# One draining step fewer between slot attention and cross attention in a fused decoder layer

## The reference

```
x = x + gated_slot_attention(layernorm(x))          # 4 heads, 64 slots
x = x + cross_attention(layernorm(x), ctx, bias)    # 16 heads of width 8
x = x + experts(layernorm(x))                       # 8 experts by LoRA, 2 chosen
# cross attention, for one batch:
scores = q k^T / sqrt(8) + attn_mask + 2 * fside    # fside: 16 x 128 x 128 per batch
scores = where(key_mask, -inf, scores)
out    = softmax(scores) v, times Wo, plus bo
```

## Time and profile before

| | us |
|---|---|
| median of 3 runs | 661.64 |
| lowest, highest | 657.6, 661.92 |
| the profiled execution: its time | 662.49 |
| its span, first to last instruction | 660.7 |
| busy: PE, DVE, ACT, POOL | 540.4, 520.1, 439.0, 366.2 |

### The profile page before, as it was taken

How to read it: one execution, slowest core, us unless ns; L and a number is a source line. 1 busy time by engine, 2 the same in 40 slices (tenths; PEclk the granted TensorE clock), 3 DMA queues, 4 the chain that set the end, 5 groups by cost and what they waited for, 6 DMA issues and landing times. The chain is left out here.

```text
span 660.7 us, 16042 instructions
## 1 busy us (share of the span) xinstructions
PE 540.4 (82%) x4272; PEld 403.4 (61%) x4272; DVE 520.1 (79%) x2036; ACT 439.0 (66%) x1569; POOL 366.2 (55%) x365
## 2 busy tenths in 40 slices
PE   3589999999999765887877887877866799999986
PEld 1357777777777643555555555555545677777764
DVE  1446878888788635999999999999986699999872
ACT  3655787787776214999999999999994232223321
POOL 5123454453543457888888888888842134333430
PEclk9778999999999755999999999999997699999999
DMA  5930000000000034788887788888700000000000
GB/s 127 213 51 1 2 0 2 0 0 0 0 1 1 3 71 83 136 152 150 148 144 136 140 153 148 151 145 141 132 2 1 0 17 16 17 16 16 17 17 16
DMA packets 87510, 42.37 MB, mean 64 GB/s; under 512 B 7466, under 2 KB 87220, under 8 KB 87476
## 3 DMA queue, kind: packets, MB, share of 16 engines
q1 hardware_dynamic: 87476, 41.97, 34.8%
HBM read 39.86 MB, written 2.10 MB: 64 GB/s over the span
## 5 line engine op out<-in xcount | busy, mean ns | idle before, releaser
L957 ACT ACTIVATE c_P<-c_P,c_min 128x128 f32<-128x128 f32 x512 | 222.0, 648 | 0.0
L957 ACT ACTIVATION_READ_ACCUMULATOR c_P<-c_P,c_min 128x1 f32 x512 | 186.8, 447 | 0.0
L1126 POOL TENSOR_TENSOR c_bias<-c_fside,c_cm 128x2048 f32<-128x2048 f32 x32 | 145.5, 4546 | 3.0 <-DVE c_cm L1043 3.0
L1018 DVE CUSTOM_DVE_ANT_0 c_P<-banks,c_bias 128x128 f32<-128x128 f32 x512 | 117.1, 286 | 7.3 <-issue 4.3
L913 PE MATMUL banks<-ident,c_P 128*128 128x128 f32 x512 | 84.1, 289 | 28.7 <-ACT c_P L957 26.1
L913 PEld LDWEIGHTS banks<-ident,c_P 128*128 128x128 f32 x512 | 57.5, 145 | 47.9 <-ACT c_P L957 31.9
L1053 DVE COPY shared<-banks 128x512 f32<-128x512 f32 x96 | 66.0, 687 | 2.8 <-PE banks L913 2.8
L1468 POOL TENSOR_TENSOR xs<-shared,xs 128x512 fp32r<-128x512 f32 x8 | 10.8, 1349 | 94.9 <-ACT xs L1300 94.9
L1233 PE MATMUL banks<-um,lb_s 128*128 128x512 f32 x192 | 56.4, 409 | 2.7 <-ACT shared L1290 1.9
L1290 ACT ACTIVATE shared<-banks,bi_col 128x512 f32<-128x512 f32 x32 | 22.0, 688 | 46.0 <-PE banks L1233 46.0
L766 POOL TENSOR_TENSOR lower<-meanvar,minus_one 128x2 f32<-128x2 f32 x16 | 3.1, 197 | 80.8 <-DVE meanvar L647 80.5
(11 more groups left out here) (195 smaller groups left out, 1451.5 us busy)
## 6 DMA issues: line engine op xcount, KB each, us to landing
c_fside<-in_fside_Bx16xSxS_dram SPq DMA_DIRECT2D x64, 512.0 KB, 7.2
X<-in_x_dram SPq DMA_DIRECT2D x4, 512.0 KB, 4.9
c_ctx<-in_ctx_dram SPq DMA_DIRECT2D x32, 64.0 KB, 5.2
out_dram<-shared SPq DMA_DIRECT2D x8, 256.0 KB, 2.3
kmask_sb<-in_mask_BxS_bf_dram SPq DMA_DIRECT2D x1, 512.0 KB, 6.9
c_P<-in_L_ffn_wi_dram SPq DMA_DIRECT2D x1, 256.0 KB
c_P<-in_L_ffn_wo_dram SPq DMA_DIRECT2D x1, 256.0 KB
c_P<-in_L_ffn_lora_B_dram SPq DMA_DIRECT2D x4, 64.0 KB
```

The lines of the kernel that those rows point to most:

```text
L957: last = nc.scalar.activation(P[:, par, h, :], P[:, par, h, :], ACT.Exp, bias=mn[:, par, h:h + 1], scale=-1.0, accum_out=rsx[:, par, h:h + 1])
L1018: last = nc.vector.tensor_tensor_reduce(out=P[:, o, h, :], in0=bank(SCORE_BANKS[i])[:, 128 * j:128 * j + 128], in1=fm[:, o, h, :], scale=- ...
L1126: nc.gpsimd.tensor_tensor(fm[:, q, :, :], fs[:, q, :, :], bc(cm[:], XH), ALU.add).then_inc(C["fm"], 1)
```

## The change

- The bias tile of batch 0 is made between slot steps 5 and 6, that of batch 1 between slot steps 14 and 15, by new functions `x_masks` (DVE) and `x_biases` (POOL) in place of the inner `masks` and `biases`. On DVE the masks stand before the loop (after step 5) and after it (before step 14).
- Cross step -3 moves ahead of slot step 16, cross -2 ahead of 17, cross -1 ahead of 18.
- In cross steps below 0, POOL does `roots` first, then `keys_apart` and the output bias, and no bias tile.
- Slot step 18 is cut: its DVE part without `mean_squares`, and POOL's squares, before cross step 0; `mean_squares` and `root` of the last pair after cross step 0; slot step 19 after cross step 1 (POOL has nothing in it).
- The fourth group of scores of batch 0 goes to bank 0 in place of bank 6; the transposes of cross step -1 then wait until all its scores are read (`C["tt"]` >= 4).

```diff
+        FIRST_BANKS = (1, 4, 5, 0)
+        def score_bank(n, i):
+            return bank((FIRST_BANKS if isinstance(n, int) and n == 0 else SCORE_BANKS)[i])
+        def x_masks(dve, k):
+            need(dve, C["fm"], k)
+            km = kmask_sb[:, bass.ds(k * T, T)]
+            nc.vector.scalar_tensor_tensor(cm[:], km, -3.0e38, half_mask[:], ALU.mult, ALU.add).then_inc(C["cm"], 1)
+        def x_biases(pool, k, m, q):
+            need(pool, C["cm"], k + 1)
+            need(pool, s_fs[q], 32 * (m + 1))
+            need(pool, C["tt"], 4 * k - 4)
+            nc.gpsimd.tensor_tensor(fm[:, q, :, :], fs[:, q, :, :], bc(cm[:], XH), ALU.add).then_inc(C["fm"], 1)
@@ x_tensor, inputs_turned
+                if isinstance(n, int) and n == -1:
+                    need(pe, C["tt"], NI)
@@ x_vector
-            if project:
-                masks()
+            if project and not (isinstance(n, int) and n < 0):
+                x_masks(dve, n + 2)
@@ x_pool
+            if isinstance(n, int) and n < 0:
+                if norm:
+                    roots()
+                if project:
+                    keys_apart()
+                    output_bias()
+                return
@@ gpsimd
             for t in range(1, 6):
                 gsa_peeled(gsa, t)
+            x_biases(pool, 0, 0, 0)
             gsa_loop(pool, gsa)
-            for t in range(PAIRS - 2, PAIRS + 1):
-                gsa_peeled(gsa, t)
+            gsa_peeled(gsa, PAIRS - 2)
+            x_biases(pool, 1, 0, 1)
+            gsa_peeled(gsa, PAIRS - 1)
             pool.wait_ge(G["xn"], PAIRS)
             x_peeled(cross, -3)
-            gsa_peeled(gsa, PAIRS + 1)
+            gsa_peeled(gsa, PAIRS)
...
             x_peeled(cross, -2)
-            gsa_peeled(gsa, PAIRS + 2)
+            gsa_peeled(gsa, PAIRS + 1)
             x_peeled(cross, -1)
-            gsa_peeled(gsa, PAIRS + 3)
-            for n in range(0, 2):
-                x_peeled(cross, n)
+            gsa(PAIRS + 2, 0, False, False, False, True, False, False, False)
+            x_peeled(cross, 0)
+            gsa(PAIRS + 2, 0, False, False, False, False, False, False, True)
+            x_peeled(cross, 1)
@@ vector
             for t in range(4, 6):
                 gsa_peeled(gsa, t)
+            dve.wait_ge(s_km, 16)
+            x_masks(dve, 0)
             gsa_loop(dve, gsa)
-            for t in range(PAIRS - 2, PAIRS + 1):
+            x_masks(dve, 1)
+            for t in range(PAIRS - 2, PAIRS):
                 gsa_peeled(gsa, t)
...
             x_peeled(cross, -3)
+            gsa_peeled(gsa, PAIRS)
+            x_peeled(cross, -2)
             gsa_peeled(gsa, PAIRS + 1)
-            dve.wait_ge(s_km, 16)
-            x_peeled(cross, -2)
-            gsa_peeled(gsa, PAIRS + 2)
             x_peeled(cross, -1)
+            gsa(PAIRS + 2, 0, False, False, False, True, True, False, False)
+            x_peeled(cross, 0)
+            gsa(PAIRS + 2, 0, False, False, False, False, False, False, True)
+            x_peeled(cross, 1)
             gsa_peeled(gsa, PAIRS + 3)
             dve.wait_ge(G["x1"], PAIRS)
-            for n in range(0, 2):
-                x_peeled(cross, n)
             x_loop(dve, cross)
@@ tensor
-            x_peeled(cross, -3)
-            gsa_peeled(gsa, PAIRS + 1)
             pe.wait_ge(G["silu"], PAIRS)
             x_peeled(cross, -2)
+            gsa_peeled(gsa, PAIRS + 1)
+            pe.wait_ge(G["shift"], PAIRS)
+            x_peeled(cross, -1)
             gsa_peeled(gsa, PAIRS + 2)
-            pe.wait_ge(G["lgts"], PAIRS)
             pe.wait_ge(G["un"], PAIRS)
-            x_peeled(cross, -1)
+            pe.wait_ge(G["onT"], PAIRS - 1)
+            pe.wait_ge(G["x1"], PAIRS - 1)
+            x_peeled(cross, 0)
+            x_peeled(cross, 1)
...
             gsa_peeled(gsa, PAIRS + 3)
             pe.wait_ge(G["x1"], PAIRS)
```

More of the change, by code:

```diff
@@ L647, in gsa_stats, with gsa_vector @@
                 nc.vector.bn_aggr(meanvar[:, b, :], stats[:, b, :]).then_inc(G["aggr"], 1)
-        def gsa_vector(dve, t, par, gate, turn, intra, mix, finish, ahead):
+        def gsa_vector(dve, t, par, gate, turn, intra, mix, finish, ahead, squares=None):
             def log_sigmoid():
@@ L754, in gsa_vector @@
                 slot_sums()
-            if mix:
+            if mix if squares is None else squares:
                 mean_squares()
@@ L773, in gsa_rstd, with gsa_pool @@
             nc.gpsimd.tensor_tensor(neg_mean[:, 0:2], lower[:, 0:2], rstd[:, 0:2], ALU.mult).then_inc(G["neg"], 1)
-        def gsa_pool(pool, t, par, gate, turn, intra, mix, finish, ahead):
+        def gsa_pool(pool, t, par, gate, turn, intra, mix, finish, ahead, norms=None):
             def heads_apart():
@@ L813, in gsa_pool @@
                 squares()
+            if mix if norms is None else norms:
                 root()
@@ L870, in all_scores @@
                     rows = slice(32 * i, 32 * i + 32)
-                    nc.tensor.matmul(bank(SCORE_BANKS[i]), qx[rows, o, :], kbd[rows, o, :, :].rearrange("p j s -> p (j s)"),
+                    nc.tensor.matmul(score_bank(n + 1, i), qx[rows, o, :], kbd[rows, o, :, :].rearrange("p j s -> p (j s)"),
                                      start=True, stop=True).then_inc(C["sc"], 1)
@@ L1017, in score @@
                     h = XG * i + j
-                    last = nc.vector.tensor_tensor_reduce(out=P[:, o, h, :], in0=bank(SCORE_BANKS[i])[:, 128 * j:128 * j + 128],
+                    last = nc.vector.tensor_tensor_reduce(out=P[:, o, h, :], in0=score_bank(n + 1, i)[:, 128 * j:128 * j + 128],
                                                           in1=fm[:, o, h, :], scale=-2.0, scalar=3.0e38, op0=ALU.add,
@@ L1037, in normalise @@
                                         ALU.subtract, ALU.mult).then_inc(C["xn"], 1)
[L1039 to L1043, removed]
             def outputs():
@@ L1119, in roots @@
                 nc.gpsimd.tensor_tensor(rstd[:, 0:1], vareps[:, 0:1], minus_half[:, 0:1], ALU.pow).then_inc(C["rstd"], 1)
[L1121 to L1126, removed]
             def keys_apart():
@@ L1677, in _ @@
                 gsa_peeled(gsa, t)
-            x_peeled(cross, -3)
-            gsa_peeled(gsa, PAIRS + 1)
             pe.wait_ge(G["silu"], PAIRS)
             x_peeled(cross, -2)
+            gsa_peeled(gsa, PAIRS + 1)
+            pe.wait_ge(G["shift"], PAIRS)
+            x_peeled(cross, -1)
             gsa_peeled(gsa, PAIRS + 2)
-            pe.wait_ge(G["lgts"], PAIRS)
             pe.wait_ge(G["un"], PAIRS)
-            x_peeled(cross, -1)
+            pe.wait_ge(G["onT"], PAIRS - 1)
+            pe.wait_ge(G["x1"], PAIRS - 1)
+            x_peeled(cross, 0)
+            x_peeled(cross, 1)
+            pe.wait_ge(C["ptD"], 6)
+            pe.wait_ge(C["ptA"], 2)
             gsa_peeled(gsa, PAIRS + 3)
             pe.wait_ge(G["x1"], PAIRS)
-            for n in range(0, 2):
-                x_peeled(cross, n)
             x_loop(pe, cross)
```

6 lines of the change are left out of this document (5 added, 1 removed).

## The result

| | median us | lowest to highest, runs | profiled run | span | first L726 to end of span |
|---|---|---|---|---|---|
| before, same session | 659.62 | 656.42 to 661.92, 4 | 662.49 | 660.7 | 595.5 |
| after | 672.72 | 671.99 to 673.12, 4 | 671.99 | 670.2 | 610.7 |

The ratio is 1.0196, interval 1.0144 to 1.0248: slower by 1.4 to 2.5%, 13.1 us by the medians where I had forecast 5.6 (667.2 us).

What follows compares the result with a forecast made beforehand. The loops leave little room (PE busy in slots, ACT in the cross loop); open time lies in the drain. -2.0 drain + 0.1 batch 3 + 0.2 masks + 4.3 hold + 3.0 clock = +5.6, so 667.2 us; range 657.5 to 674.5.

Steps and rivals of the forecast that it cites:

- the forecast case: Whole kernel: drain gives 2.0 us, slot 15's L726 is held and PE's clock falls; 661 to 671 us, chance 0.63.
- Tile 0 holds L726 too: Rival, slot 6: batch 0's tile starts before L726, so 4.3 + 3.0 us come a second time; 674.5 us, chance 0.14.
- the 0.1 for batch 3: After the drain: 0.1 us left for batch 3's scores, which start only after slot 19.
- The hold: Slot 15: batch 1's tile starts first on POOL and DVE's L726 is held until it ends; 4.3 us, bounds 0 and 4.5.
- Tile 1 hides: Rival, slot 15: batch 1's tile does not hold DVE's L726; 660.1 us, chance 0.18.
- The clock behind it: Slot 15, after held L726: PE idles, its granted clock falls to 0.50; 3.0 us, bounds 0 and 6.
- Tile 0: Slot 6: DVE's L726 starts before batch 0's bias tile and keeps 0.42 us; masks cost DVE nothing visible.
- The drain: Steps between slot and cross loops: sum 63.0 us against 65.0 before, a gain of 2.0, bounds 0 and 6.
- Cross -3: 1.9 is its full price: Drain: cross -3 keeps 1.9 us, but DVE, PE and ACT now all wait for it.
- Slot 16: 10.2, same work: Drain: slot 16, now behind cross -3, keeps its 10.2 us because its work is unchanged.
- Cross -1: 8.75: Drain: 8.75 us instead of 8.4; L871, the scores, then transposes, projections and values follow one after the other.
- Slot 19: 2.55: Drain: 2.55 us instead of 3.35, as its PE legs run at the high clock that returns in cross 0.

Runs made afterwards that it cites:

- e2: Changed kernel with PE's `mix` matmuls of slot step 15 issued five times over, same output: 667.2 us; 606.8 from first L726 to end.
- e3: Changed kernel with batch 1's bias tile made in two halves, heads 0 to 7 before L726, 8 to 15 behind: 669.0 us; 602.2 from first L726.
- e11: Same program as e1, run again for its startups: 661.1 us (2 runs) and 668.9 (4); 600.0 from first L726 to end.
- e6: e1 with slot 18 whole and slot 19 ahead of cross 0, as in the kernel before: 658.0 and 665.9 us by group, ratio 1.0010.
- e9: Changed kernel with the edits of e1, e5 and e6 together: 656.3 and 661.3 us by group, ratio 0.9963; 596.4 from first L726.
- e7: Kernel before with roots first in cross -2 and -1, batch 0's tile after slot 18's L726, batch 1's right after the roots: median 656.1 us, ratio 0.9954.
- e8: e7 with layer-norm statistics and roots of cross -2 and -1 laid inside slots 16 and 17: median 654.17 us, ratio 0.9939.
- e1: Changed kernel with one added wait: POOL makes batch 1's bias tile only after L726 of slot 15. Median 669.91 us, ratio 1.0154.
- e4: Kernel before with roots first in cross -2 and -1, batch 0's tile behind them, batch 1's after slot 19's L726: 661.78 us, ratio 1.0014.
- e5: e1 with layer-norm statistics and roots of cross -3 and -2 laid inside slots 15 and 16: 658.2 and 662.1 us by group, ratio 1.0008.

## Why the prediction was right, and where not

**The number: in the range, in part by luck.** 672.7 lies within 657.5 to 674.5, but outside the 661 to 671 that I gave the forecast case itself; the range reached so far only for the sake of the rival *Tile 0 holds L726 too*, which did not happen. Laid beside the 15.2 us of the traces, my +5.6 is 9.6 short: 0.9 in the clock behind the hold, 6.4 in the drain, 1.9 in the first loop step (2.0 against the 0.1 for batch 3), 0.4 behind it.

**The hold: right, in place and size.** Forecast: tile 1 starts first at L794's end and L726 ends with it, 4.3 us. Measured: tile 190.28, L726 190.35 to 195.06, and 4.3 by e2. What was inferred from holds of 0.6 and 1.1 us goes on to 4.5, and e3 shows it in between. The Trainium skill ("SBUF — State Buffer", Who interferes with whom), by which the first to start has the shared read port for its whole instruction, agrees. *Tile 1 hides* is out.

**The clock behind it: right, sized 3.0, measured 3.9** (e2). Granted 0.50 from 194 to 202 as forecast, and 0.69 up to 204, so it reached L701 too (its wait on ACT, behind slow PE, rose from 1.0 to 2.02).

**Tile 0: right.** At slot 6, L869 at 83.04 lets both go, L726 starts at 83.24 and takes 0.42, the tile at 83.40. The measured time lies near that rival's 674.5, but not by its mechanism. A slip that changed nothing: the rows I took for this place, at 63 to 70 us, belong to slot step 4. A second one: I said that `masks` is held by L794 to its end. It is not: in the kernel before L1043 starts at 244.62, inside L794, and takes its usual 0.28. On POOL:

```profile
244.45 1.64 POOL L794 TENSOR_TENSOR shared<-shared,minus_half 128x8 f32<-128x8 f32 x1 [0.73 <-DVE shared L720]
```

So the rule that I drew from L715 and L1404, that a DVE instruction with two inputs in SBUF is held until the POOL instruction beside it ends, is true of the add and multiply tiles here and not of this power of 8 numbers.

**The drain: the step that failed.** I summed 63.0 and measured 69.4, and forecast -2.0 where it is +4.4, with 2.0 more in the first loop step. Term by term:
- *"Cross -3: 1.9 is its full price"* and *"Slot 16: 10.2, same work"*. Cross -3 is 1.87, but it pauses PE, and slot 16 is 13.43, by 3.2 the largest miss. I charged the clock for the pause of 4.3 us and not for that of 1.9. e11 shows what the clock is worth: the same program with the clock left up takes 9.35 there. That the pause brings the fall is the likely reading (five of seven profiles with it, none of two without), but not a fixed rule.
- *Cross -1: 8.75*. It is 10.04. Start and scores together take about what I gave them (5.4 against 5.3, up to PE's first transpose at 245.06), and so do the legs from the transposes to the end of the projections, which I had read at the low clock (2.4 against 2.3, up to 247.46). What was mis-sized is the rest, "plus the values and copies": 1.1 in my sum, 2.2 measured. The values wait for ACT's copies of queries and keys, DVE's copy waits for the values, and only then come L1055 and the next L726, at 249.66:

```profile
246.83 0.63 PE L909 MATMUL banks<-c_cT,x_wT 128*128 128x128 f32 x2
248.18 0.80 PE L921 MATMUL banks<-x_wT,c_cT 128*128 128x128 f32 x2 [0.72 <-ACT c_k L992]
249.01 0.29 DVE L1086 COPY c_vpad<-banks 128x128 f32<-128x128 f32 x1 [4.11 <-PE banks L921]
```

- *Slot 17: 11.4* was 12.03, *slot 18: 8.0* 7.67, *cross 0: 8.8* 9.10, *cross 1: 8.75* 8.82: small. The late root did cost cross 1 what I said, though not all of it by the wait: L1055 waits 0.73 for its root (I had expected over 1), and L1075 before it is held 0.65 by POOL's `keys_apart`.
- *Slot 19: 2.55, "its PE legs are faster at the high clock"*. It is 3.83: DVE's L733 waits 2.64 for PE, since PE stood still at the end of cross 1 and the clock fell. The first loop step behind it takes 9.62, a cost that my sum had nowhere but in the 0.1 for batch 3: its scores on PE (L888) start 0.09 us after the step's masks and take 2.09, where before (L871, 272.15) they started 0.46 ahead and took 1.14. Late start and low clock come together here and were not tried apart. e6 takes both away and gets 2.1 back net, as the order of before has its own wait for the root.

So one mistake stands in three places, slot 16, slot 19 and the first loop step: I let durations at clock 1.00 stand behind new pauses of PE. A second one, the short chain, stands in cross -1. The bound "0, if the serial legs are longer" was too near on that side.

**Where the gain lies.** The full step that the change meant to save is worth 2 us inside the trace even with everything repaired, and nothing that the times show (e9). The 5.6 of cross -2 were real, and the kernel before can have 4.4 of them in the drain by two edits on POOL (e7), without the tiles in the slot loop; in the time of a whole run 1 to 3 us are left of that, and 3 to 4 with e8.

**Not settled.** Why the clock falls in one run and stays in another at the same pause (e1, e11) and what sets the length of the startup: the traces show the clock, not its reason. How the drain's +4.4 divides between clock and longer chains was read from the rows and not tried by itself; cross -1 took 10.0 to 10.2 in every profile of after's order, so nothing here tells what it would take at the high clock.

## What to carry to other kernels

Before an instruction of several us on GpSimd is moved into an idle gap, look at what VectorE starts in that gap with both inputs in SBUF: and whether GpSimd reaches its instruction by its own queue while VectorE waits for GpSimd's semaphore. Here GpSimd came first then (190.28 against 190.35 in after, 195.81 against 195.88 in e3), and VectorE stood for the whole instruction. The cure is one wait on GpSimd for that VectorE instruction (e1, e7); the tile starts about 0.5 us later and takes as long. And in a fill or drain, price what comes behind every new pause of TensorE at the low clock as well as at the high one, since both were seen; where two startups exist, compare intervals inside traces, or group with group, ahead of medians.

## What I had not expected of the hardware

- The hold also reaches instructions with a single tile as input: L1036 (a tile and two numbers for a partition) took 2.42 in e7 beside tile 1 (0.34 or 0.35 in the kernel before), and a plain copy, L1075 in after, 0.88 (273.99 to 274.87; 0.23 in the kernel before) beside POOL's `keys_apart` (273.74 to 274.79). The Trainium skill ("SBUF — State Buffer", Who interferes with whom) has copy and tensor_scalar among those that can take the shared ports; these two rows agree.
- Not every POOL instruction holds DVE: in before, e4, e7 and e8 the masks, two inputs in SBUF, start twice each inside `root` (L794, L814 in e8; a power of about 1.65 us) and take 0.28 every time.
- The fall of the clock is not a function of the pause alone: PE busy 2.65 of 4.00 left it at 1.00 in e11, 2.64 of 4.00 brought it to 0.50 for 8 us in e1, by the same program; 2.56 us of held L726 did not lower it in e3, 4.71 did in after. The Trainium skill ("TensorE: Matmul & The Clock Gate", Part 1) says that the gate watches activity free of the kernel's own start, so that the same work can change clock at different points; e1 and e11 agree with that, and don't prove it. e6's two groups, 7.9 us apart where before's are 6.2, and e1's, 7.8, show the same in the times.
- A pause behind the cross loop adds a spread of its own to every kernel: from the end of the first loop step to the end of the span, the same instructions in all, 380.2 us in e5, 380.4 in before, 382.6 in e1, 383.4 in e9 (granted 0.81 in 500:540 in before and e5, 0.74 in e1). A gain of 2 to 3 us in the whole of one trace can be that.
